# One instruction order for all groups and expert blocks of unequal size in a four-layer network on one core

## The reference: four layers over 128 images

```python
x = x + L0_ffn(L0_cond(x, dx, angle))      # bilinear warp; quantised 256->1024->256, gelu
x = x + L1_ffn(L1_cond(x, W1, b1, v, id))  # masked softmax pooling; 2 of 4 experts, 256->1024->256, gelu
x = x + L2_ffn(L2_cond(x, language))       # adapter 256->64->256, layernorm; frequency filter (256x256)
x = x + L3_ffn(L3_cond(x, category))       # a 256x256 matrix per image; quantised silu(gate)*up, down
```

## Time and profile before

| | before |
|---|---|
| median of 3 runs | 2972.21 us (2965.74 to 2979.16) |
| the profiled execution | 2966.13 us, its span 2963.9 us |
| mean granted TensorE clock | 0.859 of 2.4 GHz |
| busy share PE, DVE, ACT, POOL | 76%, 64%, 56%, 51% |
| instructions | 53531 |

### The profile page before, as it was taken

How to read it: one execution, slowest core, us unless ns; L and a number is a source line. 1 busy time by engine, 2 the same in 40 slices (tenths; PEclk the granted TensorE clock), 3 DMA queues, 4 the chain that set the end, 5 groups by cost and what they waited for, 6 DMA issues and landing times.

```text
span 2963.9 us, 53531 instructions
## 1 busy us (share of the span) xinstructions
PE 2259.2 (76%) x12260; PEld 1752.2 (59%) x12260; DVE 1882.2 (64%) x6227; ACT 1664.2 (56%) x2732; POOL 1520.0 (51%) x1604
## 2 busy tenths in 40 slices
PE   4002333998799889988998899979997999899655
PEld 2001212776577667766776677757775777688332
DVE  5645666666677767776777677767777754333444
ACT  0013433565477767776777577757776776445222
POOL 0366665666677656665666566656665411110110
PEclk9555555999899999999999899989998999899766
DMA  3233332443555455545554555445545543445221
GB/s 150 58 96 100 102 114 73 112 135 83 162 150 153 117 163 152 152 117 165 152 152 116 160 152 151 118 139 154 156 135 141 160 135 94 135 146 157 73 84 54
DMA packets 310735, 379.41 MB, mean 128 GB/s; under 512 B 142708, under 2 KB 246009, under 8 KB 296062
## 3 DMA queue, kind: packets, MB, share of 16 engines
q1 hardware_dynamic: 263156, 294.86, 33.1%
q0 software_dynamic: 45056, 73.48, 10.6%
q10 hardware_dynamic: 2188, 7.42, 0.6%
HBM read 291.13 MB, written 76.05 MB: 124 GB/s over the span
## 4 chain that ended last, share of the span: by engine, by line
PE 43%; SPq 14%; issue 9%; DMA 5%; DVE 3%; POOL 3%; ACT 2%; DVEq 0%; POOLq 0%; ACTq 0%
PE bank L1561 14%; PE bank L1543 12%; PE bank L1432 3%; PE bank L1426 3%; DMA adapters<-in_adapter 2%; POOL w_win L1156 2%; SPq L743 2%; PE bank L1613 2%; PE bank L1420 2%; SPq L741 1%; PE bank L1414 1%; SPq L738 1%; SPq L651 1%; PE bank L1595 1%; SPq L648 1%
## 5 line engine op out<-in xcount | busy, mean ns | idle before, releaser
L1156 POOL DMA_INDIRECT w_win<-in_windows,w_idx x1024 | 1060.1, 1035 | 655.0 <-issue 370.2
L1561 PE MATMUL bank<-moe_w,moe_hidden_T 128*128 x2816 | 681.6, 389 | 34.0 <-issue 26.7
L1543 PE MATMUL bank<-moe_xT,moe_w_tile 128*128 128x256 f32 x2816 | 679.4, 387 | 12.1 <-DMA moe_w_tile<-in_moe_w 10.3
L1561 PEld LDWEIGHTS bank<-moe_w,moe_hidden_T 128*128 128x128 f32 x2816 | 535.6, 194 | 135.8 <-issue 60.5
L1543 PEld LDWEIGHTS bank<-moe_xT,moe_w_tile 128*128 128x128 f32 x2816 | 537.1, 194 | 101.8 <-issue 28.2
L1342 ACT ACTIVATE moe_hidden_T<-bank,moe_b 128x256 f32<-128x256 f32 x704 | 295.1, 470 | 279.5 <-PE bank L1543 276.0
L811 DVE TENSOR_TENSOR w_prod<-w_win,w_hat 128x72 f32<-128x72 f32 x2048 | 313.4, 227 | 92.1 <-issue 90.7
L1342 ACT ACT_TABLE_LOAD x151 | 193.7, 1283 | 207.2 <-PE bank L1543 201.8
L1111 DVE SCALAR_TENSOR_TENSOR hidden_back<-bank,back_stats,hidden_back 128x512 f32<-128x512 f32 x128 | 95.1, 743 | 162.3 <-ACT hidden_back L1382 162.3
L1188 POOL DMA_INDIRECT moe_y_back<-moe_out_sorted,rows_back x128 | 136.0, 1063 | 117.4 <-issue 107.6
L1174 POOL DMA_INDIRECT moe_in_sorted<-c,rows x128 | 132.5, 1035 | 99.2 <-issue 65.9
(11 more groups left out here) (257 smaller groups left out, 4152.1 us busy)
## 6 DMA issues: line engine op xcount, KB each, us to landing
moe_w_tile<-in_moe_w SPq DMA_DIRECT2D x88, 1024.0 KB
L_cond_W<-in_L_cond_W SPq DMA_DIRECT2D x128, 256.0 KB
adapters<-in_adapter SPq DMA_DIRECT2D x128, 192.5 KB
moe_x<-moe_in_sorted SPq DMA_DIRECT2D x88, 256.0 KB
moe_out_sorted<-moe_y SPq DMA_DIRECT2D x88, 256.0 KB
w_win<-in_windows,w_idx POOLq DMA_INDIRECT x1024
gamma_beta<-in_gamma_beta SPq DMA_DIRECT2D x128, 128.0 KB
c<-w_out SPq DMA_DIRECT2D x512, 16.0 KB
```

The lines of the kernel that those rows point to most:

```text
L1156: gp.indirect_dma_start(out=V[:, g_ * WLEN:(g_ + 1) * WLEN], out_offset=None, in_=t["windows"], in_offset=bass.IndirectOffsetOnAxis(ap=idx ...
L1543: last = te.matmul((H0, H1)[r % 2][:, (f % 2) * TILE:(f % 2 + 1) * TILE], W1[n % 3][:, d * F + f * P:d * F + (f + 1) * P], XT[:, d * TILE: ...
L1561: last = te.matmul(Y[:, u * D:(u + 1) * D], hT[:, (f % 4) * TILE + u * P:(f % 4) * TILE + (u + 1) * P], ap(moe2, weight[n] + f * D, [[1, D ...
```

## The change: one string for each engine

The turns, the slot tables, the loop and its register arithmetic go. `weave` now takes threads that run over all 32 groups (or all 88 tiles) one after another, and follows a fixed string `ORDER` with one letter for each step of a thread; there is one string for each engine, 3832 letters on VectorE, 1880 on TensorE, 1496 on ScalarE, 1440 on GpSimd, 682 on SyncE. Letters: f front, a attend, b back, l last, e experts, w warp, p plan, g gather, s scatter, y y_back (on SyncE r is regroup, z zeros, x x_in, w an expert's weights, l a tile's rows, y moe_out, c last_in). What a step computes is as before.

```diff
-BQ = 4
-NBK = NQ // BQ
-TILES = 2 * BTOK // TILE + EXP - 1
-TURN_TILES = ((0, 1, 2), (3, 4, 5), (6, 7, 8), (9, 10))
-XROWS = EXP * BTOK + TILE
-LAG = 8
+BLOCKS = (2, 3, 5, 6, 6, 5, 3, 2)
+BFIRST = [sum(BLOCKS[:b]) for b in range(NBK + 1)]
+NTILE = [2 * n * QT // TILE + EXP - 1 for n in BLOCKS]
+TFIRST = [sum(NTILE[:b]) for b in range(NBK + 1)]
+ARENA = max(BLOCKS) * QT * EXP + TILE
-SLOT = {
...
+ORDER = {
+    "vector":
...
+    "tensor":
+        "fffffffffaaaafafafafaafffffaafafffaaaaaaffffefaeaeeefaefefeeafeeaeaeaeafeafeeefeeeeefeefeeaeaefeeeafefefeeaaeaea"
...
+    "sync":
+        "zzzmzgxxcgrrgrrgrrgrrogbbmrrxgrrgobmrrxgwwwlrrglomwlyrrxwlgryrgwloymwlrryxglrrgyomyrrxgyrrgowwwllmbwxlrrcygwolrr"
...
+def weave(eng, **threads):
+    live = {name[0]: thread for name, thread in threads.items()}
+    for thread in live.values():
+        next(thread)
+    for name in ORDER[eng]:
+        next(live[name], None)
+
+def each(thread, items):
+    for n in items:
+        yield from thread(n)
```

The expert offset is now read for every quarter of a tile on TensorE and ScalarE, ahead of the wait for the data. Every `sem_inc` on a `passed_` semaphore goes. SyncE's expert loads are two threads, so that a tile's weights are loaded ahead of its rows, and SyncE waits for the two memsets before it loads the first geometry:

```diff
                 def down_(n, k):
-                    pe.wait_ge(E["m_ev"], RING * b + 5 * n + 1 + k + 1)
-                    if k == 0:
-                        after(pe, E["m_yev"], TILES * b + n)
-                        pe.wait_ge(E["plan"], b + 1)
-                        pe.sem_inc(E["passed_t"], 1)
-                        _, (weight[n],) = nc.values_load_multi_w_load_instructions(
+                    pe.wait_ge(E["plan"], TBLOCK[n] + 1)
+                    _, (weight,) = nc.values_load_multi_w_load_instructions(
...
+                    pe.wait_ge(E["m_ev"], FILL * n + 1 + k + 1)
+                    if k == 0:
+                        after(pe, E["m_yev"], n)
...
+            def rows_in(n):
+                yield
+                sp.wait_ge(E["plan"], TBLOCK[n] + 1)
+                after(sp, E["m_fill"], FILL * (n - 1) + 1)
+                if n in TFIRST:
+                    sp.wait_ge(E["a_sc"], 64 * BFIRST[TBLOCK[n] + 1])
+                moe_rows(n)
+
+            def weights_in(n):
+                yield
+                if n == 0:
+                    for z in range(4):
+                        sp.wait_ge(s_zero[z], 16 * ZEROS)
+                sp.wait_ge(E["plan"], TBLOCK[n] + 1)
+                after(sp, E["m_fill"], FILL * (n - 2))
+                moe_weight(n)
...
+            sp.wait_ge(E["mk0"], 2)
             load_geometry(0, 0)
-            load_geometry(1, 1)
             load_offsets(0, 0)
-            sp.wait_ge(E["mk0"], 2)
-            run_turns(sp, None, 0, turn)
```

More of the change, by code:

```diff
@@ L89, in spaced @@
         n = self.base + self.n
-        yield next(at)
+        yield
         self.eng.wait_ge(self.sem, n)
-SLOT = {
[L95 to L148, removed]
-}
@@ L157, in after, with begins, ends @@
         eng.wait_ge(sem, n)
[L160 to L196, removed]
+def weave(eng, **threads):
[7 more added lines that the diff above has]
+        yield from thread(n)
+TBLOCK = [b for b in range(NBK) for _ in range(NTILE[b])]
+def begins(x):
+    return x % NU == 0 and x // NU in TFIRST
+def ends(x):
+    return x % NU == NU - 1 and x // NU + 1 in TFIRST
 BITW = ["L0_w1", "L0_w2", "L3_gate", "L3_up", "L3_down"]
@@ L1135, in _ @@
             v.tensor_copy(run[:, :], cst[:, C_BASE:C_BASE + EXP]).then_inc(E["run"], 1)
-            for _s in coords(0, 0, 0):
-                pass
-            run_turns(dve, ch, DVE_STEPS, turn)
+            q_ = range(NQ)
+            weave("vector", front=each(front, q_), attend=each(attend, q_), rows=each(fetch, q_), back=each(back, q_),
+                  last=each(last, q_), plan=each(make_plan, range(NBK)), experts=each(evict, range(GT)),
+                  warp=each(warp, q_), coords=each(coords, q_))
         @block.gpsimd
@@ L1217, in back @@
                                  ALU.add).then_inc(E["b_xf"], 1)
[L1219 to L1226 removed]
+            q_ = range(NQ)
+            weave("gpsimd", front=each(front, q_), y_back=each(y_back, q_), back=each(back, q_), scatter=each(scatter, q_),
+                  gather=each(gather, q_))
         @block.scalar
@@ L1395, in back_q2T @@
                 s.copy(Q2TB[:, :], B0b).then_inc(E["b_q2T"], 1)
-            def turn(i, j, b, w, c, a, f, sc, m, k, l):
-                par = j % 2
-                weave(a and front(i + 1, 1 - par, j), f and attend(i, j), k and back(i - LAG, j), l and last(i - LAG - 1, j),
-                      m and j == 0 and first(b, j), m and experts(b, j), c and hats(i + 3, j))
             s.activation(A2h[ADIM:ADIM + 1, :], b1B[ADIM:ADIM + 1, 0:QT], ACT.Copy, bias=1.0, scale=0.0)
-            for _s in hats(0, 0):
-                pass
-            run_turns(act, ac, ACT_STEPS, turn)
+            q_ = range(NQ)
+            weave("scalar", front=each(front, q_), attend=each(attend, q_), back=each(back, q_), last=each(last, q_),
+                  experts=each(experts, range(UNITS)), hats=each(hats, q_))
         @block.tensor
```

843 lines of the change are left out of this document (422 added, 421 removed).

## The result

The changed kernel takes 2877.94 us (median of 4 runs, 2875.12 to 2880.9) against 2972.36 us for the kernel before in the same measurement: ratio 0.9682, 95% interval 0.9658 to 0.9706. The forecast was 2840 us, so the gain is 94 us where 132 were forecast. The profiled execution has a span of 2875.6 us.

A forecast was written before the change was run, and what follows sets the result against it. PE was taken as the bound, full only in the middle, so only its idle time could move. Head 375, middle 1909, to last tile 416 and tail 131 give 2831, plus 2 and 6 about 2840 us; 8-in-10 range 2735 to 2985.

The forecast's parts named there:

- E: Sequencer work: loop removal worth nothing, at most 11 us; added register reads, dropped increments and register sums 0.
- The reads: Register reads on PE rise from one to four a tile, ahead of the data wait: taken as 0.
- rival 3: The 264 added reads on PE are uncovered and cost 79 us: 2919 us, chance 0.10.
- A: Head, to the end of attend of group 1: 375 us (345 to 410), with 15 us for the zero fills.
- the new order gives back 7 us of the second turn: In the head, before attend of group 1 ends: a 7 us gain from the order.
- B: Attend of group 1 to attend of group 31: 30 steps at 8% idle or the front's pace, 1909 us, before 2153.
- the pace of 51: Shortest step in the middle, set by the front: 51 us, the middle of 41 and 61.
- C: From attend of group 31 to the last tile: 385 us x 1.08 = 416 us (385 to 470).
- D: Tail after the last eviction: two groups fewer at 41 us each leave 131 us, before 213.
- Rival 1: The front's pace stays at 61 us and zeros cost all they can: 2987 us, no gain, chance 0.12.
- Rival 2: Strings run out of step, late waits hold up what follows: 3061 us at 20% PE idle, 2986 at 16%; chance 0.14.
- rival 4: Everything fits: pace 45 us, 5% idle, zeros hidden, tail 101: 2695 us; halfway 2765; chance 0.17 for 2700 to 2790.

The follow-up runs named there:

- unrolled: The kernel before with only its loop of four passes written out, so waits are against constants: 2941.47 us, ratio 0.9908.
- no_passed: unrolled without the 36 lines that increment `passed_` semaphores, on which nothing waits: 2915.07 us, ratio 0.982.
- turn_order: The changed kernel's code with 8 blocks of 4 groups and the old slot order: 2908.37 us, ratio 0.98; on the slow chip 3388.67 us, 0.9864.
- one_read: The changed kernel with the expert's offset read once a tile on PE and ACT instead of four times: 2875.18 us, ratio 0.9685.
- planned_equal: The changed kernel with five new strings and 8 blocks of 4 groups: 2998.56 us, ratio 1.0102; on the slow chip 3453.74 us, 1.0052.
- planned_unequal: The changed kernel with five new strings, its unequal blocks kept: 2941.18 us, ratio 0.9916; on the slow chip 3380.05 us, 0.9822.

## Why the prediction came out too low by 38 us

**Where the time came from.** The steps from 2970 us: the loop 29 (unrolled), the increments 26 (no_passed), the other code about 7 (turn_order, not clear of noise), blocks and strings 31 (the changed kernel against turn_order). The prediction put 0 to 11 us on the first three and 132 on the last. So the time is near, and the direction right, but two errors of opposite sign stand behind that: without the 55 us that it did not count, the kernel would have been near 2933 us (an estimate, 2878 + 55), outside the band of 2790 to 2900 that the forecast names, though inside its range of 2735 to 2985. That the time landed in the band is luck.

**E, what runs on sequencers is free: this step failed.** It read "register sums ran beside busy engines: 0" and gave the same 0 to the increments. They carried 55 us. Here busy neighbours were no cover for an instruction that stands between a wait and the work behind it. When the wait ends the chain, as it does at many places in a turn, each such instruction is on the path. The trace shows this for the increments on PE, where the idle time by "issue" fell; for the sums it is argued. The prediction had the number in its rows: the 26.7 us of idle time by "issue" stood behind the place of two increments, and it was ascribed to a register read. The same holds for the loop: its cost was looked for at four branches, and lay outside the steps that hold them, where the loop has its sums, 2944 of 32 to 40 ns. The Trainium skill (Runtime: NRT & Kernel Launch, Instruction fetch mechanics) names the taken branch as one reason why control flow is expensive. Here the branch was the smaller part: a 3.8 us stall in three passes, 11 us at most and hidden in the steps that hold it, against 29 us for the whole loop.

**The reads: right.** Four reads a tile cost nothing (one_read), and rival 3 falls with it; its mark, idle time by "issue" at the down projection, is 0.4 us. What differs from the increments is their place: the reads stand ahead of the data wait. That the place is the reason was not tested with a read moved behind the wait.

**A, the head: the fills were right in kind, the order was mis-sized.** Attend of group 1 ends at 339 us, not 375, and earlier than the whole range of 345 to 410. (The 4.25 MB given there for an arena before are 4.46 MB in the unit of its 6.55.) The fills ran at up to 391 GB/s, not 294: from 113 to 176 us

```profile
113.00:176.00 63.00, 0.00 (x0) 0.00 (x0) 3.81 (x18) 5.61 (x8) 30.62 (x32) 0.50 0.96 391
```

They delay front of group 0 by 36 us, but are worth 7 at the end of attend of group 1. What the prediction missed is that group 0 itself gets faster. From its first statistic to the end of attend it takes 71 us (215 to 286), where the turn tables took 127 (179 to 306). The step "the new order gives back 7 us of the second turn" held the second turn alone.

**B, the middle: this step failed, by 98 us.** The 30 steps take 2007 us, not 1909. (Their listed work adds to 1679 us, not to the 1688 given; the 1909 does follow from the list.) Split by the listed work of PE: the seven steps with 47 us of work or less were to take 51 us each, 357 together, and take 65, 53, 47, 49, 76, 47 and 64, that is 401. Four of them are at 47 to 53 us, so the pace of 51 was right there. The other three (65, 76, 64) hold a block start each, with 7.8, 16.2 and 7.8 us of wait for `moe_x`, for which B had no term; without these waits they are still at 56 to 60. PE is busy 283 us in the seven steps, where 241 were listed. The 23 other steps hold 1438 us of listed work, and PE is busy 1444 in them; they were to take 1553 and take 1606. So the work of these was sized well, and idle time is 11% of it, not 8. The 8% came from the old turns, and did not carry over to the new strings. Nor was it what the old order costs by itself: with the new code it has 6% away from block starts. Why the new strings lose more (because they never repeat, or because their order is worse) was not separated.

**C and D: right.** 411 us against 416, and 119 against 131.

**Rivals.** Rival 1 fell: the pace is 47 to 53 us in the four steps without a block start. Rival 2 was half true. Idle time in the middle is 290 us against 2095 busy, 14%, just under the break-even of 15% that the prediction worked out; by the mark that it set, away from block starts, it is 12%. The waits of PE on DVE and ACT are there, with the adapters beside them. Of rival 4 the head came true (339 us against its 355) and about half of the tail (119, between 131 and its 101), but not the middle. The mark for PE's busy time between 385 and 2700 us, 2060, came out at

```profile
385.00:2700.00 2315.00, 2024.88 (x11231) 1590.34 (x11229) 1581.15 (x5452) 1514.66 (x2492) 1337.10 (x1405) 0.94 0.48 137
```

35 us less, as the last eviction is at 2757 us and not at 2700.

## What to carry to other kernels

Look at what stands between a wait and the work behind it, on every queue of a chain. An increment there was on the path here, however idle the sequencer looked, and register sums in a loop seem to have been; reads ahead of the wait were free. A repeating table can be good in a way that is easy to miss: its low idle time inside the turns is something that a long fixed string must first reach again. When a schedule is made to fill the ends, take the idle time of the middle as a term that can grow, and compare head, middle and tail of both kernels, since what is gained at the two ends is easily given back between them.

## What was not expected of the hardware

**Increments that nobody waits for cost 26 us.** From unrolled to no_passed the semaphore events fall from 1489 to 522 on PE's queue and from 1471 to 80 on GpSimd's, by 621 on SyncE's, 179 on VectorE's and 90 on ScalarE's. Which engine's increments count most was not separated. Idle time before the down projections falls by 14.6 us, where PE's idle time from the first tile to the last eviction falls by 18.

**The order of four zero fills hardly matters.** 26 MB at the start or between the first groups differ by 7 us in a kernel of 2875 us, inside the noise, though the first makes group 0 start 38 us later.

**One chip was 16% slower than the other with the same kernel before** (3440.55 and 2970 us). Its trace of turn_order differs from the other chip's in SyncE's own small instructions. Line L668, the register moves of the mask loads, on the slow chip and then on the other (minimum/median/maximum ns):

```profile
L668 SPq MOVE mask<-in_masks x128: 5/29/897, 269.6 to 2886.3; - x128
```

```profile
L668 SPq MOVE mask<-in_masks x128: 29/29/43, 258.8 to 2422.6; - x128
```

The median is the same, 29 ns. But 159 of SyncE's 3108 register instructions (MOVE, FUSED_REGOPS, ALU_OP and SEQ_ASSERT, without the TENSOR_LOADs) took over 0.4 us, and none did on the other chip. VectorE's queue has 30 of them, TensorE's and ScalarE's none. Whether they account for the 470 us was not shown. The Trainium skill (Runtime: NRT & Kernel Launch, Instruction fetch mechanics) has instruction fetch hidden behind the rate at which an engine issues. The trace of the faster chip agrees so far as none of these instructions took over 0.19 us, and whether fetch is what stalls the other one was not tried. The ratios of turn_order and of planned_equal agree on both chips within their intervals; that of planned_unequal is 0.982 on one and 0.992 on the other, with intervals that only touch.
